# Attention scores by one product on a block diagonal of K, head average by accumulated transposes, dt in six buffers

## What is computed

```python
x = _layernorm(x + mamba(x))           # in_proj, conv of 4, silu, x_proj, softplus(dt), scan over 16 states, gate, out_proj
x = _layernorm(x + cross_attn(x, ctx)) # top-32 attention, FiLM, a long convolution over positions, an MLP
x = _layernorm(x + routed_ffn(x))      # mix of neighbours, nine small experts
```

```python
Q = (x_text @ Wq).reshape(Bb, Tt, H, DH)          # H, DH = 4, 32
K = (x_vision @ Wk).reshape(Bb, Gg, H, DH)
scores = jnp.einsum('bthd,bghd->bhtg', Q, K) / np.sqrt(DH)
scores = jnp.where(vision_mask[:, None, None, :], scores, -jnp.inf)
topv, topi = jax.lax.top_k(scores, K_TOP)         # K_TOP = 32
attn = zeros.at[..., topi].set(softmax(topv))
attn_mean = attn.mean(axis=1)                     # over the 4 heads
```

## Time and profile before

| | us |
|---|---|
| median of 3 runs | 7286.86 |
| lowest, highest | 7278.25, 7288.03 |
| the profiled execution | 7288.94 |
| its span | 7287.1 |
| share of the span busy: TensorE, weight loads, VectorE, ScalarE, GpSimd | 92%, 51%, 74%, 61%, 63% |
| mean granted TensorE clock | 0.955 |

### The profile page before, as it was taken

The page is one execution under the profiler, slowest core; times in us unless marked ns, Lnnn a source line. Parts: engine busy times, 40 slices in busy tenths (PEclk is TensorE's granted clock), DMA queues, the critical chain, the costliest instruction groups (busy, mean ns, idle before and its releaser), DMA issues. The chain is left out here.

```text
span 7287.1 us, 107870 instructions
## 1 busy us (share of the span) xinstructions
PE 6717.7 (92%) x25168; PEld 3749.4 (51%) x25168; DVE 5404.4 (74%) x13962; ACT 4452.2 (61%) x9788; POOL 4596.0 (63%) x3991
## 2 busy tenths in 40 slices
PE   3899999999999999999999999997789999999997
PEld 1354455554555444454445554554656666666664
DVE  5588888888888888888888888886336666666665
ACT  2788888788887888878888788885212212221111
POOL 0788888888888888888888888897011111111111
PEclk6999999999999999999999999998789999999998
DMA  1556556665566656656556565555611111111110
GB/s 41 137 146 150 137 143 157 148 151 142 143 154 154 145 142 142 148 153 149 143 137 152 157 149 145 139 154 170 204 36 35 32 32 32 32 32 32 32 32 20
DMA packets 554213, 835.19 MB, mean 115 GB/s; under 512 B 169179, under 2 KB 207388, under 8 KB 551712
## 3 DMA queue, kind: packets, MB, share of 16 engines
q1 hardware_dynamic: 552768, 820.23, 44.5%
q10 hardware_dynamic: 864, 8.65, 0.3%
HBM read 745.91 MB, written 74.45 MB: 113 GB/s over the span
## 5 line engine op out<-in xcount | busy, mean ns | idle before, releaser
L1255 POOL TENSOR_TENSOR arena<-arena 128x512 f32<-128x512 f32 x2048 | 2588.2, 1279 | 308.3 <-DVE arena L1180 258.6
L877 PE MATMUL psum<-arena 128*128 128x512 f32 x4096 | 2156.2, 622 | 30.0 <-POOL arena L1255 24.0
L1180 DVE TENSOR_TENSOR_SCAN arena<-arena,psum 128x512 f32<-128x512 f32 x1024 | 1236.4, 1207 | 379.5 <-ACT arena L1049 292.6
L1268 POOL TENSOR_TENSOR arena<-arena 128x512 f32<-128x512 f32 x1024 | 1334.5, 1303 | 121.8 <-PE psum L877 121.4
L1036 ACT ACTIVATE arena<-arena 128x128 f32<-128x128 f32 x4096 | 1301.8, 394 | 141.6 <-PE psum L862 141.0
L1184 DVE TENSOR_TENSOR_SCAN arena<-psum,arena 128x512 f32<-128x512 f32 x1024 | 1234.4, 1205 | 86.7 <-issue 38.7
L877 PEld LDWEIGHTS psum<-arena 128*128 128x128 f32 x4096 | 703.9, 197 | 570.0 <-issue 379.4
L1834 POOL TENSOR_SCALAR arena<-arena 128x4 f32<-128x4 f32 x160 | 36.8, 230 | 1164.9 <-DVE arena L1695 1164.9
L1049 ACT ACTIVATE arena<-arena 128x508 f32<-128x508 f32 x1024 | 735.9, 719 | 57.9 <-DVE arena L1180 57.1
L862 PEld LDWEIGHTS psum<-arena 128*128 128x128 f32 x4096 | 515.5, 146 | 492.9 <-issue 438.5
L1049 ACT ACTIVATE psum<-arena 128x508 f32<-128x508 f32 x1024 | 699.7, 683 | 50.5 <-DVE arena L1180 31.0
(11 more groups left out here) (218 smaller groups left out, 10304.8 us busy)
## 6 DMA issues: line engine op xcount, KB each, us to landing
arena<-bc_scratch SPq DMA_DIRECT2D x1152, 512.0 KB, 5.2
arena<-in_xT_dram SPq DMA_DIRECT2D x32, 512.0 KB
arena<-in_x_dram SPq DMA_DIRECT2D x32, 512.0 KB, 7.7
x_scratch<-arena SPq DMA_DIRECT2D x32, 512.0 KB, 5.6
xin_scratch<-arena SPq DMA_DIRECT2D x128, 128.0 KB, 2.5
arena<-kernel_scratch SPq DMA_DIRECT2D x32, 512.0 KB, 6.4
arena<-x_scratch SPq DMA_DIRECT2D x32, 512.0 KB, 3.7
out_dram<-arena SPq DMA_DIRECT2D x32, 512.0 KB
```

The costliest lines, as they stand in the source:

```text
L877: pe.matmul(y_ps, ident, ring[:, u % RING], start=False, stop=n == NS - 1).then_inc(S["nsum"], 1)
L1180: dve.tensor_tensor_scan(s, decay_sb[:, u // 2 % 2], bx_ps[:, u // 2 % 2], 0.0, ALU.mult, ALU.add)\
L1255: pool.tensor_tensor(h, h, Cb[:, u // 2 % PAIRS, u % 2], ALU.mult).then_inc(S["hc"], 1)
L1268: pool.tensor_tensor(ring[:, u % RING], uu[par][:, c], Bb[:, state(u)], ALU.mult)\
```

## The change

K is no longer kept as one tile `kT` but in `kz`, [128, 4 sequences, 4 heads, 128], zero except that head h's 32 partitions are filled in head h's columns. ScalarE fills it with four copies of 32 partitions instead of one of 128; VectorE zeroes the tile once, at the start. A sequence's scores are then one mask product of 512 columns and one f32 product of 128 rows and 512 columns, without waits between heads.

The head weights multiply the masked scores in place (`sc`) instead of the identity, and the average is four transposes that accumulate in PSUM. The tile `diag` is gone. ScalarE's `dg` waits for the masking (`em`) in place of the average before.

dt has six buffers of 512 columns instead of eight: groups 0 and 1 are shared by consecutive blocks, for which `dt0` and `dt1` on ScalarE wait for the decays of the block before. xs moves next to uu. At the end of pass 1 SP's loads for pass 2 (`load_toeplitz`) wait for other semaphores, since other tiles now lie there. Semaphore counts follow. No table of places changes.

```diff
--- before.py
+++ after.py
@@ -80,8 +80,8 @@
     vabs=4, vrelu=4, vexp=1, w1=1, rest=1, vln=1, ds_mm=4, dt=4, u=4,
     decay=64, bx=32, bxt=32, bxp=32, scan=64, hc=64, nsum=64, y=4, yg=4,
     o_mm=2, res=2, st1=4, mv1=1, ve1=1, rs1=1, nm1=1, nb1=1, x1=4, st2=4, mv2=1, ve2=1, rs2=1, tmb=1,
-    xt_mm=2, x1T=2, q_mm=1, k_mm=1, qT=1, kT=1, maskb=1, s_mm=16,
-    v8=4 * KR, took=4 * KR, nmax=4, ex=4, em=4, rinv=4, rq=4, diag=4, at_mm=4, atT=4,
+    xt_mm=2, x1T=2, q_mm=1, k_mm=1, qT=1, kT=H, maskb=1, s_mm=G,
+    v8=4 * KR, took=4 * KR, nmax=4, ex=4, em=4, rinv=4, rq=4, scaled=4, at_mm=4, atT=4,
     xa_mm=2, xaT0=1, xaT1=1, film_mm=4, film_mul=4, film=4,
 )
 
@@ -505,10 +506,11 @@
         ring = cv.f32(RING * T).rearrange("p (s t) -> p s t", s=RING)
         assert cv.at <= SCAN_COLS
         cv.at = SCAN_COLS
-        dt, uu = [], []
+        uu, xs = [], []
         for _ in range(2):
-            dt.append(cv.f32(C * T).rearrange("p (c t) -> p c t", c=C))
             uu.append(cv.f32(C * T).rearrange("p (c t) -> p c t", c=C))
+            xs.append(cv.f32(C * T).rearrange("p (c t) -> p c t", c=C))
+        dt6 = cv.f32((C + 2) * T).rearrange("p (c t) -> p c t", c=C + 2)
         win = cv.f32(DH * 2 * DI).rearrange("p (k e) -> p k e", k=DH)
         wxp = cv.f32(C * 96).rearrange("p (c r) -> p c r", c=C)
         wdt = cv.f32(DI, R)
@@ -537,10 +538,10 @@
         xn = xn_x1T[:, 0:G * D].rearrange("p (b d) -> p b d", b=G)
         x1T = xn_x1T[:, G * D:].rearrange("p (k t) -> p k t", k=DH)
         small = xn_x1T.rearrange("p (c t) -> p c t", c=C)
-        qT, kT = cv.f32(T), cv.f32(T)
+        qT = cv.f32(T)
+        kz = cv.f32(G * H * L).rearrange("p (b h g) -> p b h g", b=G, h=H)
         sc = cv.f32(H * P).rearrange("p (h g) -> p h g", h=H)
         left = cv.f32(H * P).rearrange("p (h g) -> p h g", h=H)
-        diag = cv.f32(H * P).rearrange("p (h g) -> p h g", h=H)
         at = cv.f32(T).rearrange("p (b t) -> p b t", b=G)
         xa0, xa1 = cv.f32(T), cv.f32(T, CT2 + 1)
         stats = cv.f32(G * 6).rearrange("p (b s) -> p b s", b=G)
@@ -552,6 +553,12 @@
 
         decay_ps, bx_ps, score, y_ps, side = psum[:, 0:2], psum[:, 2:4], psum[:, 4], psum[:, 5], psum[:, 6:8]
         score_h = score.rearrange("p (h g) -> p h g", h=H)
+
+        def dt(par, c):
+
+            return dt6[:, c if c < C // 2 else c + C // 2 * par]
+
+        assert ACT_AT["dt0"] >= NS and ACT_AT["dt1"] >= 2 * NS
 
         def uT(par, c):
             return uT5[:, c if c < C - 1 else C - 1 + par]
@@ -694,8 +701,7 @@
             store_rest(NB - 2)
             store_xin(NB - 2)
             load_back(NB - 1)
-            need_apart(sp, ("decay", NB - 2, C * NS), ("u", NB - 1, C), ("scan", NB - 2, C * NS), ("ut_mm", NB - 1, C))
-            need(sp, "bx", NB - 2, 32)
+            need_apart(sp, ("nsum", NB - 2, C * NS), ("bx", NB - 2, 32))
             for k in range(TOEP):
                 load_toeplitz(sp, kr_d, sh, 0, k)
             need_apart(sp, ("nsum", NB - 1, C * NS))
@@ -811,26 +817,19 @@
                     if b == 0:
                         need(pe, "em", i - 1, G)
                         need(pe, "qT", i, 1)
-                        need(pe, "kT", i, 1)
+                        need(pe, "kT", i, H)
                         need(pe, "maskb", i, 1)
                     else:
                         need(pe, "em", i, b)
-                    for h in range(H):
-                        rows = slice(h * HD, (h + 1) * HD)
-                        if h:
-
-                            need(pe, "s_mm", i, b * H + h)
-                        o, row = ps[:, h * P:(h + 1) * P], slice(h * HD, h * HD + 1)
-                        pe.matmul(o, ones[row], maskb[row, b * L:(b + 1) * L], start=True, stop=False)
-                        pe.matmul(o, qT[rows, b * L:(b + 1) * L], kT[rows, b * L:(b + 1) * L],
-                                  start=False, stop=True).then_inc(S["s_mm"], 1)
+                    pe.matmul(ps, ones[0:1], maskb[0:1, b * L:(b + 1) * L][:, None, :].to_broadcast([1, H, L]),
+                              start=True, stop=False)
+                    pe.matmul(ps, qT[:, b * L:(b + 1) * L], kz[:, b], start=False, stop=True).then_inc(S["s_mm"], 1)
                 elif name[:2] == "at":
                     b = int(name[-1])
                     ps = bank(f"a{b}")
-                    need(pe, "em", i, b + 1)
-                    need(pe, "diag", i, b + 1)
+                    need(pe, "scaled", i, b + 1)
                     for h in range(H):
-                        mm = pe.matmul(ps[:, 0:L], sc[:, h], diag[:, h], start=h == 0, stop=h == H - 1)
+                        mm = pe.matmul(ps[:, 0:L], sc[:, h], ident, start=h == 0, stop=h == H - 1, is_transpose=True)
                     mm.then_inc(S["at_mm"], 1)
                 elif name == "xa":
                     for n, (lo, hi) in enumerate(((0, P), (P, CTX))):
@@ -949,9 +948,11 @@
                         need(act, "st_xin", i - 3, 64)
                         need(act, "q_mm", i - 2, 1)
                         need(act, "u", i - 2, C)
+                    if c < C // 2:
+                        need(act, "decay", i - 1, NS * (c + 1))
                     act.activation(small[:, c], tile_ps(name), ACT.Abs, bias=vec[:, V_DTB + c:V_DTB + c + 1])\
                         .then_inc(S["vabs"], 1)
-                    act.activation(dt[par][:, c], tile_ps(name), ACT.Relu, bias=vec[:, V_DTB + c:V_DTB + c + 1])\
+                    act.activation(dt(par, c), tile_ps(name), ACT.Relu, bias=vec[:, V_DTB + c:V_DTB + c + 1])\
                         .then_inc(S["vrelu"], 1)
                 elif name == "se":
 
@@ -980,10 +981,12 @@
                         act.copy(x1T[:, k], tile_ps(f"t{k}")).then_inc(S["x1T"], 1)
                 elif name == "qk":
                     need(act, "q_mm", i, 1)
-                    need(act, "s_mm", i - 1, G * H)
+                    need(act, "s_mm", i - 1, G)
                     act.copy(qT, tile_ps("q")).then_inc(S["qT"], 1)
                     need(act, "k_mm", i, 1)
-                    act.copy(kT, tile_ps("k")).then_inc(S["kT"], 1)
+                    for h in range(H):
+                        rows = slice(h * HD, (h + 1) * HD)
+                        act.copy(kz[rows, :, h], seqs(tile_ps("k"))[rows]).then_inc(S["kT"], 1)
                 elif name == "y3":
                     read_y(i, C - 1)
                 elif name[:2] == "sm":
@@ -1000,13 +1003,10 @@
                     need(act, "tmb", i, 1)
                     act.activation(rq, rinv, ACT.Identity, scale=tmb[:, c:c + 1]).then_inc(S["rq"], 1)
                     need(act, "rq", i, c + 1)
-                    if c:
-                        need(act, "at_mm", i, c)
-                    else:
-                        need(act, "at_mm", i - 1, G)
+                    need(act, "em", i, c + 1)
                     for h in range(H):
-                        a = act.activation(diag[:, h], ident, ACT.Identity, scale=rq[:, h:h + 1])
-                    a.then_inc(S["diag"], 1)
+                        a = act.activation(sc[:, h], sc[:, h], ACT.Identity, scale=rq[:, h:h + 1])
+                    a.then_inc(S["scaled"], 1)
                 elif name[:2] == "at":
                     need(act, "at_mm", i, c + 1)
                     if c == 0:
@@ -1073,6 +1073,7 @@
                 act.activation(diag_d[:, c], ident, ACT.Identity, scale=vec[:, V_D + c:V_D + c + 1])\
                     .then_inc(diag_made, 1)
             act.wait_ge(zeroed, 4)
+            act.wait_ge(kz_zero, 1)
             for s in [s for s in ACT_AT if s in FRONT]:
                 step(s, 0, 0)
             for u in range(ACT_AHEAD):
@@ -1130,9 +1131,9 @@
                     if r:
                         need_apart(dve, ("took", i, n))
                     elif b:
-                        need_apart(dve, ("s_mm", i, (b + 1) * H), ("nmax", i, b))
+                        need_apart(dve, ("s_mm", i, b + 1), ("nmax", i, b))
                     else:
-                        need_apart(dve, ("s_mm", i, H))
+                        need_apart(dve, ("s_mm", i, 1))
                     for h in range(H):
                         a = dve.max(v8[:, r, h], src[:, h])
                     a.then_inc(S["v8"], 1)
@@ -1193,6 +1194,7 @@
 
             dve.memset(xa1[CT2:CT2 + 1], 1.0).then_inc(bias_one, 1)
             dve.memset(ones, 1.0).then_inc(bias_one, 1)
+            dve.memset(kz, 0.0).then_inc(kz_zero, 1)
             for k in range(2):
                 dve.memset(seqs(decay_ps[:, k])[:, :, 0:1], 0.0).then_inc(zeroed, 1)
                 dve.memset(seqs(decay_sb[:, k])[:, :, 0:1], 0.0).then_inc(zeroed, 1)
```

14 lines of the change are left out of this document (7 added, 7 removed).

## The result

The changed kernel takes **7304.86 us** (median of 8 runs, 7303.24 to 7316.38), the kernel before in the same comparison 7287.03 (8 runs, 7274.47 to 7292.06). The ratio is 1.0024, with a 95% interval of [1.0016, 1.0033]: slower by some 18 us. On another chip the two stood at 7304.84 and 7278.56, ratio 1.0037 [1.0023, 1.0051]. The forecast was 7263, some 24 us faster; the time went the other way, though the range up to 7325 holds it. Two executions of one variant further down (`k_split`), at 7995 and 9768 us with a granted clock of 0.82 and 0.65 over the whole span, are left out of its time.

A forecast was written before the change was run, and what follows sets the result against it. Path: k projection, ScalarE's queue, TensorE's queue to the y sum, ScalarE again, plus the clock; GpSimd from step 43. 30 blocks x (1.44-1.03-1.06 = -0.65) = -19.5, tail -4.5: -24.0 us, so 7263 us; range 7215 to 7325.

The forecast's parts named there:

- second score: Second sequence's scores (step 29) by one mask and one f32 product: -1.03 us a block, on the path.
- TensorE's queue to the y sum: Part of the claimed path: TensorE runs without a gap from the bc copy through the second score to L1027's sum.
- k copies: Three more k copies on ScalarE before the bc copy, 0.48 us each: +1.44 us a block, on the path.
- first score: First sequence's shorter score: nothing, since it waits for the fourth k copy and TensorE would wait for silu anyway.
- GpSimd's full stretch: From about step 43 to 63 GpSimd is busy 39.30 of 39.3 us, so it sets the pace there.
- The clock: Clock falls after the second score vanish, as its product is dense and half as long: -1.06 us a block.
- fourth score: Fourth sequence's shorter score lies in GpSimd's full stretch: nothing, up to 1.0 more gain if that cover is less tight.
- last average: Last of a block's four head averages, by transposes, in GpSimd's full stretch: 0, at most -0.45 us.
- rival 4: TensorE counts in more places: fourth score (1.03) and last average (0.45) pass through, 44 us less, 7219; chance 0.15.
- xs's move at 0: xs's buffer moves next to uu; the prediction names no term for this move.
- Rival 2: TensorE newly waits some 1.7 us for silu at L746 and the clock falls there: 7311, long falls 7360; chance 0.15.
- Rival 3: More transposes in the last averages lower the clock once per block: 45 us, 7308; chance 0.05.

The follow-up runs named there:

- k_split: Changed kernel with decay 24 ahead of the k copies, two of them on ScalarE and two on VectorE between scans 23 and 24: 7318.5 us, ratio 1.0043.
- four_pairs128: Changed kernel with its score product taken apart into four pairs, each waiting for the one before, on all 128 rows: 7357.9 us (one run).
- old_scores: Changed kernel with k in one copy and the four score pairs of the kernel before: 7284.2 us, ratio 1.001.
- one_copy: Changed kernel with one k copy of 128 partitions instead of four of 32 (scores not the reference's): 7242.5 us, ratio 0.9954.
- xs_back: Changed kernel with xs's buffer back at its old place and zs beside uu: 7285.9 us, ratio 1.0008.
- avg_only: Kernel before with only the head average by four transposes instead of eight half products: 7252.5 us, ratio 0.9957.
- dt6_only: Kernel before with only dt in six buffers and xs next to uu: 7285.0 us, ratio 0.9993.
- rows32: Changed kernel with its one f32 score product on 32 rows only, those of head 0: 7304.2 us (one run).
- one_mask: Kernel before with the average by transposes and one 128-row mask product of 512 columns ahead of a sequence's four serial 32-row products: 7251.1 us, ratio 0.996.
- pad16: Changed kernel with 16 more idle waits on TensorE's queue, once, ahead of the loop over the blocks: 7349.2 us, ratio 1.0088.
- dense_mask: Kernel before with the average by transposes and each small mask product on all 128 rows (weights 1/128) instead of one: 7346.2 us, ratio 1.0094.

## Why the prediction was wrong, point by point

**The second score: the step that weighs most.** The prediction put its saving on the path, -1.03 us a block, because "TensorE's queue to the y sum" was taken as the path from the bc copy to the y copy. A score did get shorter (0.84), but the saving is worth nothing there: in blocks without a fall 25-34 and 34-43 are as long as before (0.01 more, and 26.94 to 26.97 us in all four profiles), and the y copy follows scan 25 by 17.6 us either way. TensorE was busy without a gap in that stretch and still had slack. It holds the scans up when it is slower: at half the clock, and with the four waiting pairs of `four_pairs128` (27.6 us in blocks without a fall behind the second score).

**The k copies: mis-sized, and their followers missed.** The term was 3 x 0.48 = +1.44, on ScalarE's queue up to the bc copy. The copies take 1.81 more in block 16 (0.48 was the spacing of 128-partition copies; these start 0.60 apart). Three more things stood behind them: the decay of step 24, the first score with the top-32, and the decay of step 25. The prediction said VectorE's wait for scores is not on the path, "since GpSimd's full stretch follows". In fact a delay of VectorE at scan 25 arrives whole (25-34 is 0.01 in nearly all kernels, and 34-43 does not make it good). The first score, taken at nothing, was worth -0.68 with one copy, and the copies took that back too. The copies' price: 62 us instead of 43.

**The clock: right.** -1.06 a block was forecast from one profile, where 11 blocks fell; the falls go to 0, and 34-43 is 1.32 shorter against the mean of two profiles, with 11 and 15. A short fall cost 1.6 us and a long one 3.2, as the prediction took them. From `old_scores` to `one_copy` the whole score part is 42 us, although the first column goes against it by 0.90 a block: fewer falls 1.13, first score 0.68. The table's sum, 0.92 a block, makes 28 of them; another 10 lie in blocks 29 to 31.

**The fourth score: rightly at nothing.** It shows -0.75 in 43-47 and is given back by scan 55, as the prediction's full GpSimd says: 43 to 55 adds up to 0.14 in the changed kernel and 0.16 with the old pairs, to -0.39 in `xs_back` and -0.41 in `avg_only`, which has the old pairs too. **The last average: wrongly at nothing.** Four transposes do take the 0.44 us that the prediction took for them (2736.19 to 2736.63 in the changed kernel's block 16), and of the 0.45 saved 0.41 passes (0.19 where xs lies at its new place: 0.35 in `dt6_only`, 0.16 in `old_scores`). Here GpSimd's 39.30 of 39.3 us did not mean that only GpSimd set the pace, and rival 4 was right in this half; by which path it passes is open.

**xs's move at 0: wrong.** It costs 0.18 us in each of four products, and 0.53 a block between scans 52 and 55 (0.35 without the new average).

**Rival 2** gave a time near the result for a reason that did not occur: its waits came, the falls did not (0 of 26). Where such falls were brought about, in `rows32` and `k_split`, they cost 0 and 0.4 us, not 1.6. Rival 3 did not occur.

**The jump** was in no case of the prediction. It holds 0.55 a block of the 0.69: 0.5 us in the crossing to the next block and 0.6 from its scan 0 to 6, at every second block. Over the 13 jumps that is some 14 us of the 18, and two profiles of the same kernel differ by 0.15 and 0.3 a block there, so a part of it may be scatter. Without it the change would be nearly neutral: what the falls and the average give, the copies and xs take (0.14 a block is left, 4 us).

Sum for a block: further copies 1.91, first score -0.68, falls of the clock -1.32, last average -0.39, xs 0.53, first column 0.36, 55-64 0.25 (the jump, all but 0.06): 0.66, times 30 blocks 20 us. The forecast's was 1.44 - 1.03 - 1.06 = -0.65. The 1.3 between them: 2.6 more from the second score (1.03), the columns of the jump (0.61), xs (0.53) and the copies (0.47), and 1.3 less from the first score (0.68), the average (0.39) and the falls (0.26).

## What to carry to other kernels

An engine in order has two kinds of followers behind an added instruction: the work it feeds and whatever else stands in its queue. List both, and for each ask whether the receiver has slack up to the next stretch. An engine that shows busy without a gap may still have slack: compare the marks of another engine with and without the saving. Add up neighbouring stretches before a gain in one of them is believed. Before small gains are credited to an edit, compare what no edit touches: here a loop's jump made most of the difference between the two kernels, and eight idle instructions moved it by 44 us. Of the parts measured here the average alone, at 7252.5 us, is the version to keep, level with `one_mask`; but only 0.41 us a block (12 us) is shown to be the average's own, and what the jump gives may go with the next edit.

## What was not expected of the hardware

- TensorE stands still behind the jump of a loop for 0 to 3.2 us at a time, and with the same work it depends on where the code lies (block 16 of `dt6_only`, before, changed, `pad16`: 0, 1.46, 1.57 and 1.48, 3.21).
- GpSimd's product of two 128x512 f32 operands takes 1099 or 1276 ns by where the operands lie (of its two operands only xs lies elsewhere in `xs_back` and in the changed kernel).
- Copies out of PSUM of 32 partitions x 512 on ScalarE follow each other every 0.6 us, as against 0.48 for 128 partitions; on VectorE two take 1.42 us.
- Four transfers of 64 KB within SBUF take 2.76 us to issue on one queue, and the product that waits for the last starts 6.9 us after the first issue.
- The clock fell more often when the four mask products used 128 rows than when they used one (25 of 26 blocks against 5, `dense_mask` and `avg_only`).
